# A macaron block's causal attention: the mask as a selection on GpSimd over the exponentials, diagonal units of equal width, values weighed in quarters, constants and first loads reordered

## The chip, the cores and the metric

One core of a Trainium2 chip runs the whole program. The metric is the device time of one launch in microseconds, the median over runs. Engines: TensorE (PE) multiplies, VectorE (DVE), ScalarE (ACT) and GpSimd (POOL) work on elements, and SyncE (SP) issues most DMAs. Each engine runs its own list of instructions in order; they wait for each other by semaphores.

## The reference

x has 4 sequences of 2048 rows of width 256. The block is x + 0.5 ffn(ln(x)), then + attention(ln(x)), then + 0.5 ffn(ln(x)); both feed-forward parts are a routed mixture of 8 experts and are not touched here. The attention, 16 heads of 16 with 4 nodes each:

```
node_probs = softmax(x @ Wr)                       # 4 nodes per head and row
pos = cumsum(node_probs) - node_probs              # positions for the rotation of q and k
scores = (q_r @ k_r.T) * SCALE + log(node_probs @ node_probs.T + 1e-08)
attn = softmax(where(causal, scores, -inf))        # key row <= query row
x + (attn @ v) @ Wo
```

The kernel takes the logarithm out of the softmax: exp(score) is multiplied by the sum over nodes of p_query * p_key. So the values are weighed beforehand by each of the 4 key nodes (`val`, 16 values and the weight itself, 17 columns per node, 68 per key row), and the 4 node sums are put together with the query's p afterwards.

## The kernel before

`build_attention` stands between two calls of `build_ffn`; nothing overlaps across them. 8192 rows are 64 tiles of 128, taken in pairs (TP = 32). Each pair goes through about ten steps per engine: normalise, transpose, project to v and node logits, softmax, sums before (positions), sine and cosine, rotate, split q and k in three bf16 parts, store these to DRAM, project the next q and k. Five pairs are made ahead, in `lead`; the others, and the output projections of finished rows, are slotted into the attention's unit loop at fixed steps of a *turn* (4 short turns of 24 units, then long ones of 40; the lists SHORT_AT and LONG_AT on each engine give the steps).

A *unit* is one head, 512 queries (CH = 4 tiles of 128) and two tiles of 128 keys. A head has 4 chunks of queries; chunk c has 2c full units and then two diagonal units, 20 units per head, 1280 in all, 512 of them diagonal. Scores are held keys down, queries across: tile `4c + t` of the keys meets the queries from t on, (4 - t) * 128 columns. Before, the first diagonal unit holds t = 0 and 1 (512 + 384 = 896 columns), the second t = 2 and 3 (256 + 128 = 384). A *visit* loads the q and k parts of two heads for chunks 0 and 1 (12 units), or of one head for chunks 2 and 3 (14 units); 96 visits.

For unit u: `scores(u)` on TensorE (L1568) fills `ring[u % 2]` in PSUM; on the first 128 columns of each diagonal tile two more matmuls (two halves of 64 keys) add -1e30 where the query is earlier than the key, as `ident_b` times `late_kq` (L1582 to L1585). `weights(u)` on ScalarE (L1181) writes the exponentials to `ew[u % 5]`. `weighted(u)` on TensorE (L1588) multiplies each 128 by 128 block of them with the 68 value columns, adding up a chunk in `mix[block % 2]`; each matmul here shows as two records in the trace, so a full unit has 32, the diagonal ones 28 and 12. `mix_nodes` on VectorE (L1435) finishes a chunk.

TensorE's order (L1778): at unit u it issues scores(u + 2), which waits for the exponentials of u, then weighted(u - 1), then the step of the turn. In a long turn, at step 0 and from step 26 (BURST) on, it also issues weighted(u), directly behind.

GpSimd (L1087) makes constants, `val` of the next visit (`weigh_values`, once per head and visit, at the visit's third unit) and the sums `acc`. Its constants are one chain; `consts_ready` is raised once, behind the last (L1110). VectorE, TensorE and ScalarE wait for it at their very start (L1295, L1565, L1163); ScalarE waits for all weights besides, scales Wq and Wk (L1168), loads the table and only then does `rsqrt(0)`. SP loads five weights, then the first x (L996 to L999).

Of the kernel before, what the change touches and what calls it, by code (L numbers as in the profile page):

```python
# [7 lines left out]
BF16 = mybir.dt.bfloat16  # L8
# [709 lines left out]
def build_attention(nc, x, Wq, Wk, Wv, Wr, Wo, q_parts, k_parts, B):  # L718
# [53 lines left out]
    for n, (v, e, i) in enumerate(stints):  # L772
# [10 lines left out]
    first_unit.append(U)  # L783
    block_of = [sum(1 for e in end_of if e < u) for u in range(U)]
# [17 lines left out]
    def place(u, n):  # L802

        n0, c, j, t0 = units[u]
        if j < CH * c:
            return 0, n * 512
        return (n, n * 512) if t0 == 0 else (2 + n, n * 256)

    def width(u):

        t, at = place(u, 1)
        return at + (CH - t) * P
# [31 lines left out]
    with ExitStack() as ctx:  # L844
# [15 lines left out]
        late_kq = sb("late_kq", [P, P], BF16)  # L860
# [69 lines left out]
        names = ("consts_ready pool_step dve_step act_step w_loaded w_scaled x_loaded var_ready rs_ready xn_ready xnT_ps "  # L930
# [60 lines left out]
        with nc.Block() as block:  # L991

            @block.sync
            def _(sp):
                sp.sem_inc(s["shift_loaded"], 32)
# [3 lines left out]
                sp.dma_start(xin[:, :, :], x_v[0]).then_inc(s["x_loaded"], 16)  # L999
# [88 lines left out]
            def _(pool):  # L1088
                ch = Chain(pool, s["pool_step"])
                identity(pool, ch, ident[:, :])  # L1090
                ch(pool.tensor_copy(ident_b[:, :], ident[:, :]))
                ch(pool.tensor_scalar(minus_b[:, :], ident[:, :], -1.0, None, ALU.mult))
# [3 lines left out]

                for m, a in ((late_kq, 1), (late_qk, -1)):
                    ch(pool.memset(m[:, :], 0.0))
                    ch(pool.affine_select(out=m[:, :], in_=m[:, :], compare_op=ALU.is_ge, fill=NEG,
                                          base=0, pattern=[[a, P]], channel_multiplier=-a))  # L1100
                ch(pool.memset(ones[:, :], 1.0))
                for f in range(NF):
                    ch(pool.memset(freq_t[:, f, :], freq[f]))
                    ch(pool.memset(cos1[:, f, :], float(np.cos(freq[f]) - 1.0)))
                    ch(pool.memset(sin1[:, f, :], float(np.sin(freq[f]))))
                ch(pool.memset(half_pi[:, :], PI / 2))
                for q in range(2):
# [21 lines left out]
                def weigh_visit(v):  # L1129
                    for n, (w, e, i) in enumerate(stints):  # L1130
                        if w == v:
                            weigh_values(n)
# [732 lines left out]
```

## Time and profile before

| | |
|---|---|
| median of 3 runs | 2971.42 us (2971.05 to 2972.08) |
| the profiled execution, its own time | 2976.97 us |
| its span in the profile | 2975.2 us |
| first ffn / start and lead of the attention / unit loop / second ffn | to 368 / to 562.4 / to 2594 / to 2975.2 us |
| busy: TensorE, VectorE, ScalarE, GpSimd | 2504.0, 1720.2, 1664.8, 644.3 us |

Times within the profile count from the start of the span. A group "x32" in a timeline merges instructions of one form that follow each other; "[0.40 <-PE ...]" is the idle time of the engine before it and what ended it. Matmuls overlap in the pipeline, so a mean duration is longer than the distance between two starts; the busy time of a group is the union. PEclk is the granted TensorE clock as a share of full speed.

### The profile page before, as it was taken

The page shows a single profiled execution, that of the slowest core. Times are in us where ns is not written, and L with a number is a line of the kernel's source. Part 1 is how long each engine was busy: PE and PEld are TensorE (multiplying, and loading weights), DVE is VectorE, ACT ScalarE, POOL GpSimd, SP SyncE. Part 2 cuts the span into 40 slices and gives each one's busy share as a digit, 9 for nine tenths or more (in the row PEclk, how much of TensorE's full clock was granted, in tenths as well). Part 3 has the DMA queues.
Part 4 walks back from the last instruction along what each step waited for, and adds up shares of the span by engine and source line. Part 5 has one row for each costly group of instructions (what it writes and reads, how often), then busy time and mean ns, then how long its engine had stood idle before and what let it go on. Part 6 is the DMA issues. An engine that isn't in the chain of part 4 may idle for free. (4 is left out here: it accounts for less than half of the span.)

```text
span 2975.2 us, 107297 instructions
## 1 busy us (share of the span) xinstructions
PE 2504.0 (84%) x48010; PEld 1968.7 (66%) x48012; DVE 1720.2 (58%) x3589; ACT 1664.8 (56%) x2102; POOL 644.3 (22%) x657
## 2 busy tenths in 40 slices
PE   7287535588899999999999989999999999962876
PEld 4155312366678888778888777888878888841554
DVE  7733158788666657767656776656575222267331
ACT  6022123355577777767777766777776666660221
POOL 1078710111011111111111111111111111010787
PEclk9598866799999999999999999999999999985988
DMA  6455501121212112211111221111122111161555
GB/s 226 134 102 102 79 29 30 47 60 40 58 52 60 45 51 73 69 48 56 56 52 51 78 64 52 59 52 48 58 75 65 46 46 46 44 234 25 98 101 75
DMA packets 185116, 207.46 MB, mean 70 GB/s; under 512 B 35984, under 2 KB 151712, under 8 KB 184480
## 3 DMA queue, kind: packets, MB, share of 16 engines
q1 hardware_dynamic: 158880, 165.60, 18.5%
q0 software_dynamic: 24576, 34.10, 7.2%
q8 instruction: 407, 6.67, 0.9%
q14 instruction: 101, 0.83, 0.1%
q10 hardware_dynamic: 1152, 0.26, 0.0%
HBM read 131.68 MB, written 76.02 MB: 70 GB/s over the span
## 5 line engine op out<-in xcount | busy, mean ns | idle before, releaser
L1186 ACT ACTIVATE at_ew<-at_ring 128x1024 f32<-128x1024 f32 (+2 forms) x1280 | 1114.9, 898 | 401.5 <-PE at_ring L1580 229.7
L1604 PEld LDWEIGHTS at_mix<-at_val,at_ew 128*64 128x64 f32 x34816 | 1210.0, 138 | 194.5 <-issue 43.2
L1604 PE MATMUL at_mix<-at_val,at_ew 128*64 128x68 f32 x34816 | 1258.9, 224 | 28.4 <-DVE at_mixed L1440 28.1
L1580 PE MATMUL at_ring<-at_qT,at_kT 98*64 98x512 bf16 (+3 forms) x5120 | 729.5, 352 | 55.5 <-ACT at_ew L1186 35.8
L1440 DVE TENSOR_TENSOR at_mixed<-at_mix,at_prob 128x272 f32<-128x272 f32 x256 | 112.4, 439 | 457.3 <-PE at_mix L1604 455.1
L1122 POOL TENSOR_TENSOR at_val<-at_prob,at_eps_t 128x32 f32<-128x32 f32 (+1 forms) x128 | 49.4, 386 | 1411.1 <-PE at_mix L1604 1411.1
L1580 PEld LDWEIGHTS at_ring<-at_qT,at_kT 98*64 98x64 bf16 x5120 | 255.8, 111 | 128.1 <-ACT at_ew L1186 45.5
L328 POOL DMA_INDIRECT out_dram<-ffn_xn,ffn_idx_all x128 | 212.6, 1661 | 53.2 <-issue 34.1
L1125 POOL TENSOR_TENSOR at_val<-at_vo,at_val 128x512 f32<-128x512 f32 (+1 forms) x128 | 211.4, 1652 | 10.0
L1660 PE MATMUL at_side<-at_w_all,at_turned 128*64 128x512 f32 (+1 forms) x1024 | 200.5, 536 | 11.9 <-ACT at_vo L1206 4.3
L1584 PE MATMUL at_ring<-at_late_kq,at_ident_b 128*64 128x128 bf16 x2048 | 204.9, 222 | 0.0
L318 POOL DMA_INDIRECT ffn_xn<-table,ffn_idx_all x128 | 123.2, 963 | 311.7 <-DMA ffn_idx_all<-ffn_idx_hi 273.6
L392 ACT ACTIVATE ffn_w1T<-ffn_pair 128x512 f32<-128x512 f32 x16 | 9.6, 597 | 297.0 <-PE ffn_pair L677 297.0
L1443 DVE TENSOR_REDUCE at_summed<-at_mixed 128x68 f32<-128x272 f32 x256 | 161.4, 630 | 8.8
L577 DVE TENSOR_SCALAR ffn_xn<-ffn_bank,ffn_slot_score 128x256 f32<-128x256 f32 x128 | 62.0, 484 | 177.5 <-PE ffn_bank L705 157.7
L1380 DVE TENSOR_REDUCE at_sums<-at_prods 128x512 f32<-128x2048 f32 x64 | 146.1, 2282 | 2.5 <-issue 1.2
L1660 PEld LDWEIGHTS at_side<-at_w_all,at_turned 128*64 128x64 f32 x1024 | 70.1, 144 | 104.4 <-issue 65.3
L1584 PEld LDWEIGHTS at_ring<-at_late_kq,at_ident_b 128*64 128x64 bf16 x2048 | 120.9, 113 | 7.5 <-issue 3.9
L697 PE MATMUL ffn_bank<-ffn_xn,ffn_w1T 128*128 128x512 f32 x256 | 120.7, 626 | 0.9 <-issue 0.9
L685 PE MATMUL ffn_pair<-ffn_ident,ffn_xn 128*128 128x128 f32 x256 | 50.5, 377 | 79.7 <-DMA ffn_xn<-table,ffn_idx_all 79.1
L705 PE MATMUL ffn_bank<-ffn_w2T,ffn_xn 128*128 128x256 f32 x512 | 116.8, 384 | 0.0
L1445 DVE TENSOR_TENSOR at_vo<-at_summed,at_recip 128x64 f32<-128x64 f32 x256 | 111.2, 434 | 8.8
(227 smaller groups left out, 2790.3 us busy)
## 6 DMA issues: line engine op xcount, KB each, us to landing
table<-ffn_xn SPq DMA_DIRECT2D x32, 512.0 KB, 6.3
q_parts<-at_parts SPq DMA_DIRECT2D x64, 192.0 KB, 2.5
k_parts<-at_parts SPq DMA_DIRECT2D x64, 192.0 KB, 3.0
at_qT<-q_parts SPq DMA_DIRECT2D x128, 96.0 KB
at_kT<-k_parts SPq DMA_DIRECT2D x64, 192.0 KB
ffn_front<-in_L_attn_x_dram SPq DMA_DIRECT2D x16, 512.0 KB, 5.5
ffn_w_in<-in_L_ffn_w_dram SPq DMA_DIRECT2D x32, 256.0 KB, 3.7
at_xin<-out_dram SPq DMA_DIRECT2D x32, 256.0 KB, 5.4
```

Of the source, the lines that this page charges most:

```text
L318: pool.indirect_dma_start(out=rows[e % 2][:, j, :], out_offset=None, in_=table, in_offset=bass.IndirectOffsetOnAxis(ap=idx_all[:, e * J + ...
L328: pool.indirect_dma_start(out=dst, out_offset=bass.IndirectOffsetOnAxis(ap=idx_all[:, e * J + j:e * J + j + 1], axis=0), in_=y[e % 2][:, j ...
L697: last = pe.matmul(bank[n % 2][:, :], w1T[q][:, k, f * P:(f + 1) * P], xeT[:, k, s * 512:(s + 1) * 512], start=(k == 0), stop=(k == DK - 1))
L705: last = pe.matmul(bank[2 + j % 2][:, 0:D], hT[:, f, j * P:(j + 1) * P], w2T[q][:, f, :], start=(f == 0), stop=(f == FK - 1))
L1125: pool.tensor_tensor(val[q][:, tiles, :, 0:HD], vv.unsqueeze(2).to_broadcast([P, nk, K, HD]), val[q][:, tiles, :, HD].unsqueeze(3).to_broa ...
L1186: act.activation(ew[u % NE_BUF][:, 0:w], ring[u % 2][:, 0:w], ACT.Exp).then_inc(s["exp_ready"], 1)
L1380: ch(dve.tensor_reduce(sums[:, n:n + 2, :].rearrange("p c n -> p (c n)"), prods[:, n:n + 2, :].rearrange("p c (n k) -> p (c n) k", k=K), A ...
L1443: ch(dve.tensor_reduce(summed[:, :, :], mixed[:, :, :, :].rearrange("p t k w -> p t w k"), AX.X, ALU.add))
L1580: lastm = pe.matmul(ring[u % 2][h:h + HALF, at:at + w], kT[q][:, kc + n * P + h:kc + n * P + h + HALF], qT[q][:, qc + t * P:qc + 512], sta ...
L1584: lastm = pe.matmul(ring[u % 2][h:h + HALF, at:at + P], ident_b[:, h:h + HALF], late_kq[:, :], start=False, stop=True)
L1604: lastm = pe.matmul(mix[block_of[u] % 2][h:h + HALF, t * K * VW:(t + 1) * K * VW], ew[u % NE_BUF][:, col + h:col + h + HALF], val[q][:, ti ...
L1660: lastm = pe.matmul(side[h:h + HALF, g * 512:g * 512 + n], turned[0][:, g * DK + k, h:h + HALF], w_all[:, k, first:first + n], start=(k == ...
```

## The change

- `late_kq` and its 2048 matmuls go. `mask_late(u)` on GpSimd waits for the exponentials of a diagonal unit and sets to 0, in one selection over two pieces of 128 columns in `ew`, those with the query before the key. It raises `masked`.
- The diagonal units hold t = 0 and 3 (columns 0 to 640) and t = 1 and 2 (columns 128 to 768), 640 columns each. `weighted` does the blocks off the diagonal first, then waits for `masked` and does the two on it.
- Values are weighed for four key tiles at a time (256 columns), at four units of the visit before; the node weights of all its heads come ahead of the first quarter.
- Constants: `consts_ready` rises three times: identity; then `before`, `ones`, the frequency constants (without waits between them), `half_pi`, `ident_b`, `minus_b`; last `eps_t`, the rows of `qT` and `kT`, and `late_qk`. Each engine waits where it first needs one. ScalarE loads its table first and does `rsqrt(0)` ahead of the weights. SP issues x first.

```diff
-            units += [(n, c, 2 * p, 0) for p in range(2 * c)] + [(n, c, CH * c, 0), (n, c, CH * c + 2, 2)]
+            units += [(n, c, 2 * p, None) for p in range(2 * c)] + [(n, c, CH * c, (0, 3)), (n, c, CH * c, (1, 2))]
...
+    def tile_pair(u):
+        n0, c, j, late = units[u]
+        if late is None:
+            return [(j + n, 0, n * 512) for n in range(2)]
+        return [(j + t, t, at) for t, at in zip(late, (0, 512) if late == (0, 3) else (P, 512))]
...
 SP:
+                sp.dma_start(xin[:, :, :], x_v[0]).then_inc(s["x_loaded"], 16)
                 sp.sem_inc(s["shift_loaded"], 32)
...
-                sp.dma_start(xin[:, :, :], x_v[0]).then_inc(s["x_loaded"], 16)
...
 GpSimd:
+                ch(pool.memset(ident[:, :], 0.0))
+                pool.affine_select(out=ident[:, :], in_=ident[:, :], compare_op=ALU.not_equal, fill=1.0,
+                                   base=0, pattern=[[-1, P]], channel_multiplier=1).then_inc(s["consts_ready"], 1)
...
+                pool.tensor_scalar(minus_b[:, :], ident[:, :], -1.0, None, ALU.mult).then_inc(s["consts_ready"], 1)
...
+                def mask_late(u):
+                    pool.wait_ge(s["exp_ready"], u + 1 + PRIME_S)
+                    at, size = (0, 512) if units[u][3] == (0, 3) else (P, 384)
+                    late = ew[u % NE_BUF][:, at:at + 2 * size].rearrange("p (n c) -> p n c", c=size)[:, :, 0:P]
+                    pool.affine_select(out=late, in_=late, compare_op=ALU.is_ge, fill=0.0,
+                                       base=0, pattern=[[0, 2], [1, P]], channel_multiplier=-1).then_inc(s["masked"], 1)
...
                 def unit(u, at, short, new, fin, post):
-                    if u - 2 in first_unit:
-                        v = first_unit.index(u - 2) + 1
-                        if 1 < v < V:
-                            weigh_visit(v)
+                    if u in late_of:
+                        mask_late(u)
+                    v = visit_of[u] + 1
+                    part_at = (2, 3, 8, 9) if len(visits[v - 1][0]) == 2 else (2, 3, 7, 9)
+                    if 1 < v < V and u - first_unit[v - 1] in part_at:
+                        part = part_at.index(u - first_unit[v - 1])
+                        if part == 0:
+                            weigh_nodes(v)
+                        weigh_values(v, part)
...
 ScalarE:
-                act.wait_ge(s["w_loaded"], 16 * 5)
-                act.wait_ge(s["consts_ready"], 1)
                 act.sem_inc(s["exp_ready"], PRIME_S)
+                act.preload_act_table_set("natural_log_exp_and_others")
...
+                rsqrt(0)
+                act.wait_ge(s["w_loaded"], 16 * 5)
...
 TensorE, weighted(u):
+                    whole = [(j, t, at + (t - first) * P) for j, first, at in tile_pair(u) for t in range(first + late, CH)]
+                    for n, (j, t, col) in enumerate(whole):
+                        lastm = add(j, t, col, begin and n == 0, False)
+                    if late:
+                        pe.wait_ge(s["masked"], late_of[u] + 1)
+                        for n, (j, t, at) in enumerate(tile_pair(u)):
+                            lastm = add(j, t, at, False, u in end_of and n == 1)
```

## Rows read from the trace of the kernel before

**Rows 1.** Busy us by stretch: PE, PEld, DVE, ACT, POOL, PEclk, DMA share, GB/s

```profile
562.40:771.40 209.00, 167.26 (x3218) 130.08 (x3220) 163.20 (x315) 116.33 (x157) 27.23 (x33) 0.91 0.19 54
771.40:2236.50 1465.10, 1436.69 (x32663) 1179.71 (x32661) 981.35 (x1827) 1061.08 (x1284) 197.26 (x226) 0.99 0.20 58
2236.50:2594.00 357.50, 352.66 (x8999) 306.29 (x8996) 97.87 (x205) 243.82 (x275) 45.21 (x40) 1.00 0.17 48
```

**Rows 2.** Waits of PE in 762 to 2594: us, times, longest

```profile
PE at_mix L1604 <- DVE at_mixed L1440: 28.1, 17, 5.2
...
PE at_ring L1580 <- ACT at_ew L1186: 3.2, 6, 1.0
```

**Rows 3.** Timeline of the attention's start: start us, us, engine, line, operation

```profile
368.43 0.20 POOL L49 MEMSET at_ident<- 128x128 f32 x1 [6.66 <-POOLq L228]
...
370.98 0.47 SPq L999 DMA_DIRECT2D at_xin<-out_dram  x1
...
383.75 0.10 POOL L1110 MEMSET at_eps_t<- 128x1 f32 x1
...
383.97 1.33 ACT L1168 ACTIVATE at_w_all<-at_prods 128x256 f32<-128x256 f32 x4 [41.07 <-POOL at_eps_t L1110]
...
385.08 0.17 DVE L1306 TENSOR_SCALAR at_var<-at_mv 128x2 f32<-128x2 f32 x1
...
386.85 0.20 ACT L1179 ACTIVATE at_rs<-at_logv 128x2 f32<-128x2 f32 x1
...
388.76 1.09 PE L1652 MATMUL at_side<-at_ident,at_xn 128*128 128x128 f32 x4 [39.36 <-DVE at_xn L1319]
389.89 0.60 ACT L1195 ACTIVATE at_turned<-at_side 128x512 f32<-128x512 f32 x1 [2.83 <-PE at_side L1652]
```

**Rows 4.** Groups by form: busy us, mean ns, idle before

```profile
L1186 ACT ACTIVATE at_ew<-at_ring 128x896 f32<-128x896 f32 x256 | 235.4, 919 | 90.4 <-PE at_ring L1584 90.0
...
L1584 PE MATMUL at_ring<-at_late_kq,at_ident_b 128*64 128x128 bf16 x2048 | 204.9, 222 | 0.0
...
L1099 POOL TENSOR_SCALAR_AFFINE_SELECT at_late_kq<-at_late_kq 128x128 bf16<-128x128 bf16 x1 | 0.3, 292 | 0.1
```

**Rows 5.** Timeline of PE at one pair of diagonal units

```profile
1502.06 0.22 PE L1584 MATMUL at_ring<-at_late_kq,at_ident_b 128*64 128x128 bf16 x2
1502.12 0.33 PE L1580 MATMUL at_ring<-at_qT,at_kT 98*64 98x384 bf16 x2
...
1503.40 0.22 PE L1584 MATMUL at_ring<-at_late_kq,at_ident_b 128*64 128x128 bf16 x2
1503.46 0.22 PE L1580 MATMUL at_ring<-at_qT,at_kT 98*64 98x128 bf16 x2
```

**Rows 6.** Timeline: exponentials and value product of a diagonal unit in a burst

```profile
1139.09 1.30 ACT L1186 ACTIVATE at_ew<-at_ring 128x896 f32<-128x896 f32 x2
...
1140.52 1.00 PE L1604 MATMUL at_mix<-at_val,at_ew 128*64 128x68 f32 x28
```

**Rows 7.** Timeline: GpSimd beside two operations of VectorE

```profile
1201.38 2.29 DVE L1374 TENSOR_TENSOR at_prods<-at_cs,at_g_t 128x2048 f32<-128x2048 f32 x1
...
1201.78 1.99 POOL L1122 TENSOR_TENSOR at_val<-at_prob,at_eps_t 128x32 f32<-128x32 f32 x1 [14.22 <-PE at_mix L1604]
...
1203.70 2.29 DVE L1380 TENSOR_REDUCE at_sums<-at_prods 128x512 f32<-128x2048 f32 x1
...
1203.85 1.10 POOL L1125 TENSOR_TENSOR at_val<-at_vo,at_val 128x512 f32<-128x512 f32 x1
...
1204.90 0.25 POOL L1122 TENSOR_TENSOR at_val<-at_prob,at_eps_t 128x32 f32<-128x32 f32 x1
```

**Rows 8.** Timeline: L1445 on VectorE alone, and beside a GpSimd product

```profile
1141.56 0.23 DVE L1445 TENSOR_TENSOR at_vo<-at_summed,at_recip 128x64 f32<-128x64 f32 x1
...
1509.04 2.02 POOL L1125 TENSOR_TENSOR at_val<-at_vo,at_val 128x1024 f32<-128x1024 f32 x1
...
1509.97 1.18 DVE L1445 TENSOR_TENSOR at_vo<-at_summed,at_recip 128x64 f32<-128x64 f32 x1
```

More of the change, by code:

```diff
@@ L783, in build_attention @@
     first_unit.append(U)
+    visit_stint = [n for n, (v, e, i) in enumerate(stints) if e == 0]
+    visit_of = [stints[n][0] for n, c, j, late in units]
     block_of = [sum(1 for e in end_of if e < u) for u in range(U)]
@@ L800, in blocks_until, with columns, vals_until @@
         return 1 + max(block_of[u] for u in end_of if stints[units[u][0]][2] // H == b and units[u][1] == c)
[L802 to L812, printed above, removed]
+    def tile_pair(u):
[3 more added lines that the diff above has]
+        return [(j + t, t, at) for t, at in zip(late, (0, 512) if late == (0, 3) else (P, 512))]
+    def columns(u):
+        first, last = tile_pair(u)
+        return first[2], last[2] + (CH - last[1]) * P
+    late_of = {u: n for n, u in enumerate(u for u in range(U) if units[u][3] is not None)}
+    def vals_until(stint):
+        return sum(1 + shape_of(v)[3] // CH for v, e, i in stints[:stint])
     NP = max(len(p) for p in pieces)
@@ L1095, in _ @@
                                       base=0, pattern=[[1, P]], channel_multiplier=-1))
[L1097 to L1100, printed above, removed]
                 ch(pool.memset(ones[:, :], 1.0))
                 for f in range(NF):
-                    ch(pool.memset(freq_t[:, f, :], freq[f]))
-                    ch(pool.memset(cos1[:, f, :], float(np.cos(freq[f]) - 1.0)))
-                    ch(pool.memset(sin1[:, f, :], float(np.sin(freq[f]))))
+                    ch.add(pool.memset(freq_t[:, f, :], freq[f]))
+                    ch.add(pool.memset(cos1[:, f, :], float(np.cos(freq[f]) - 1.0)))
+                    ch.add(pool.memset(sin1[:, f, :], float(np.sin(freq[f]))))
                 ch(pool.memset(half_pi[:, :], PI / 2))
+                pool.wait_ge(s["consts_ready"], 1)
+                ch(pool.tensor_copy(ident_b[:, :], ident[:, :]))
+                pool.tensor_scalar(minus_b[:, :], ident[:, :], -1.0, None, ALU.mult).then_inc(s["consts_ready"], 1)
+                ch(pool.memset(eps_t[:, :], EPS))
                 for q in range(2):
@@ L1150, in unit @@
                 def unit(u, at, short, new, fin, post):
[L1151 to L1154 removed]
+                    if u in late_of:
[5 more added lines that the diff above has]
+                        if part == 0:
+                            weigh_nodes(v)
+                        weigh_values(v, part)
                     if at == (10 if short else 14) and new is not None:
@@ L1598, in weighted, with add @@
                         pe.wait_ge(s["u_taken"], block_of[u] + 1)
[L1599 to L1608 removed]
+                    def add(tile, t, col, first, last):
+                        for h in range(0, P, HALF):
+                            m = pe.matmul(mix[block_of[u] % 2][h:h + HALF, t * K * VW:(t + 1) * K * VW],
+                                          ew[u % NE_BUF][:, col + h:col + h + HALF],
+                                          val[q][:, tile0 + tile, :, :].rearrange("p k w -> p (k w)"),
+                                          start=first, stop=last, skip_group_check=True)
+                        return m
+                    late = u in late_of
+                    whole = [(j, t, at + (t - first) * P) for j, first, at in tile_pair(u) for t in range(first + late, CH)]
[5 more added lines that the diff above has]
+                            lastm = add(j, t, at, False, u in end_of and n == 1)
                     lastm.then_inc(s["av_done"], 1)
```

102 lines of the change are left out of this document (43 added, 59 removed).

## The prediction

> **What bounds the kernel now.** I read the stretches first. The attention's unit loop is 562.4 to 2594.0, two thirds of the span. TensorE is busy for 1436.7 of 1465.1 us in its middle and for 352.7 of 357.5 at its end; ScalarE there is at 72% and 68%, VectorE at 67% and 27% [rows 1]. The list of waits says what its pauses from 762 on are: 28.1 us for VectorE and 3.2 us for exponentials [rows 2]. So in 771.4 to 2594.0 a TensorE instruction that goes away shortens the kernel by its pitch. The loop's head, 562.4 to 771.4 (the four short turns), is another case: TensorE has 167 busy us of 209, VectorE 163, and the two wait for each other through ScalarE [rows 1]. Third, 368.4 to 388.8 in the timeline: over 20 us before the attention's first matmul, in most of which GpSimd alone works [rows 3].
>
> **The start of the attention.** Before: GpSimd makes its constants one after another from 368.43 until the memset of `eps_t` ends at 383.85, and only that releases ScalarE (383.97) and VectorE [rows 3]. The four memsets of `qT` and `kT` hold it last. Input x is issued sixth, at 370.98. Then: statistics, weight scaling and a table load ahead of rsqrt (done 387.05), normalisation, first transposes 388.76 [rows 3].
> After: x is issued first, near 368.5. Its issue row at 370.98 shows it behind five weights; I let it land by 372.3, an estimate that leaves 3.8 us. Statistics end 1.4 us after their release (383.85 to 385.25), rsqrt is two instructions like the one of 0.20, 0.45 together, with the table already loaded, normalisation runs from 387.05 to 388.76, 1.7 us [rows 3]. That gives transposes at about 375.8, done at 376.9. Beside it ScalarE waits for five weights, whose last issue stays at about 371.0; with 4.4 us for issue and landing (estimate) it scales until 376.8, and copies the transposed tile then. Both arms meet near 376.8 where before they met at 389.9. **Gain 13 us.** Bounds 10 (a landing 3 us later) and 15 (neither arm late). `before`, `ident_b` and `half_pi` come by about 376 and are wanted 12 us later; the last constants (the four memsets, then `late_qk`) by about 385 and are wanted at the first visit, 150 us later. What is late next is the weights' landing. The five lead steps behind it are one chain, shift as a whole, and keep their length. SP's other DMAs keep order.
>
> **TensorE loses the mask matmuls.** Per pair of diagonal units four tiles take a second accumulation: 256 pairs, 2048 matmuls. Their mean of 222 ns is not their price [rows 4]: they are pipelined, and the two halves of a tile run together. From start to start: 1502.06 to 1502.12 and 1503.40 to 1503.46, so 0.06 us for two [rows 5]; 128 columns at the upper clock level, 2.4 GHz, which rows 1 show granted (0.99 and 1.00), say 0.053. I take 0.057. 1024 pairs come to 58 us. 64 of the 512 diagonal units lie in the four short turns (7.3 us), where TensorE does not bound; I credit half, 3.6. The rest, 51.1 us, is credited whole. Score columns and value matmuls stay as many: 512+384 and 256+128 columns become twice 640, exponentials too. Two halves alike should even ScalarE's pace; with 3.2 us of waits for exponentials left [rows 2] I price that at nothing.
>
> **GpSimd gets 512 selections.** The nearest row is a selection over 128 columns, 292 ns [rows 4]. Twice 128 columns are wanted: at least 0.29, twice that is 0.58, and a two-input operation over 512 columns, 1.10 us when free, is the far end. I take 0.45, near the first, since the fixed part is paid once.
> Does TensorE wait for it? The changed value product does its unmasked blocks first. I measured in the timeline, for every diagonal unit, the time from its exponential's end to where the last 8 value records start. Outside bursts TensorE is a unit behind: 337 units, at least 1.7 us, medians 3.4 and 3.9. In bursts (step 26 on and step 0 of a long turn) 175 units, least 1.07, median 2.05. The least: the 896-wide exponential that starts 1139.09 ends 0.92 later at 1140.01; its 28 value records start 1140.52 and take 1.0, so the last eight start near 1141.1 [rows 4, 6]. The shorter scores and the smaller unit take about 0.25 off. 0.45 plus two handovers of about 0.1 fits in 0.85: undisturbed, no unit waits.
> Disturbed it does. A GpSimd operation that meets `L1374` on VectorE is held: `L1122`, 0.25 us when free, took 1.99 from 1201.78 until L1374 was over; beside the reduction L1380 the 512-column operation took its free 1.10 [rows 7]. L1374 (2.29 us) runs twice in a row per long turn, at step 30, in the burst. In the 23 long turns that have it 24 diagonal exponentials end inside it and too late for 0.5 us of masking; their overdue times add to 22.5 us, and with neighbours that share one stall I count **15 us lost**. Bounds: 0 (other alignment, since all that follows is earlier) and 47 (0.8 us a selection, 0.6 us less slack: 50 units late).
> On this the Trainium skill, page "SBUF — State Buffer" (section "SBUF: two separate sides"), says: VectorE operations with two SBUF inputs or in a two-port mode and GpSimd operations hold a shared port pair exclusively, and the loser blocks fully. The trace agrees (1.99 against 0.25). By a split of bandwidth instead, the loss would be near 0 and the sum 15 us lower.
> It works both ways: `L1445` took 1.18 us instead of 0.23 while a GpSimd product ran [rows 8]. 512 selections of 0.45 with a third of VectorE's time in such operations delay VectorE by some 30 us in all, of which 7 in the short turns. Where TensorE bounds, VectorE has 480 us spare [rows 1]: free. In the short turns I charge 4, and 2 at the turns where value sums of short rows make TensorE wait for L1440. Bounds 0 and 15.
>
> **Queues.** In GpSimd's queue a selection can stand behind a quarter of the values (256 columns, about 0.64 by 0.18 + 0.46, from 1.10 and 2.02 for 512 and 1024 [rows 7, 8]). The quarters lie at steps 2, 3 and 7, 8 or 9 of a visit, which are full units, so no selection is due beside them; extra fixed costs, 4 times 0.2 a visit, are GpSimd's own: it is 13% busy [rows 1], with the selections some 25%. `add_up` stands behind the selection of its unit. The node weights wait for the previous visit's last product, behind the selections that this product needs: no circle. Values are ready by step 10 and wanted at 12 or 14. All nothing; if the quarters came late, a visit's start would wait, 94 times.
>
> **Sum**, against the profiled execution: 2976.97 - 13 - 3.6 - 51.1 + 15 + 6 = 2930.3. The median of the runs shown is 5.5 lower, 2971.42, so about 2925, 1.6% less.
>
> **Rivals.**
> (a) *Only the start gains.* The mask matmuls hid in TensorE's shadow, ScalarE or VectorE set the pace, or stalls eat it all: 2971.4 - 13, about 2958. For it: VectorE at 67% and the exclusion. Against it: TensorE's 98 and 99% [rows 1].
> (b) *Slower: the selection itself outlasts the slack.* At 0.9 us 6 units wait, at 1.6 63 (25 us), at 2.0 161 (78), at 2.5 208 (168), without VectorE's holds. It decides from about 1.8 us, where stalls reach the 64 us of gain less the holds; at 2.5, with 512 selections barring VectorE too, 2971 - 68 + 168 + 20 gives about 3090; at 2.0 about 3000. Against it: 292 ns for half the columns.
> (c) *No stalls*: 2971.4 - 71, about 2901, if GpSimd slips between or L1374 rarely meets a diagonal.
>
> **Numbers.** Main 0.66, with its own range 2912 to 2940; (c) 0.12; (a) 0.15; (b) 0.07. A measurement here tells 0.2%, 6 us, from no change. Faster by more: main, (c), most of (a), 0.87; within: 0.06, the far end of (a), where stalls also take the start's gain; slower 0.07. Range 2900 to 2960.
>
> **What will show it.** First attention transposes near 376 instead of 388.8. No L1584. The loop from 771 on about 36 to 50 us shorter, the short turns as long as before within 5. Selections of 0.4 to 0.5 us, some stretched to 2 or more beside L1374; TensorE's new waits on them in the bursts, some 20 of a microsecond. Wrong if selections average over 0.8 us, if TensorE's waits for them exceed 40 us, if ScalarE's waits for scores vanish (it would then bound), or if the start still waits for GpSimd.

## The result and the profile after

The changed kernel takes 2936.30 us (median of 4 runs, 2933.87 to 2937.91); the kernel before, beside it on the same chip, 2971.75 us. The ratio is 0.9876 with the interval 0.9859 to 0.9893: 1.2% or some 35 us less, where 46 were forecast. The profiled execution after has 2933.87 us against 2976.97 before, 43 us apart. It lies 2.4 below its median and that of before 5.2 above the median of 2971.75, so some 8 us of what the profiles differ by is scatter between executions.

The same stretches after (columns as in [rows 1]): the four short turns, the middle of the unit loop, its end; then one plain turn, and the two turns 10 and 11, in which new rows are brought in.

```profile
555.80:756.60 200.80, 157.50 (x2962) 120.11 (x2964) 164.00 (x315) 116.89 (x156) 77.42 (x112) 0.92 0.20 56
756.60:2203.70 1447.10, 1399.48 (x31233) 1138.52 (x31231) 981.19 (x1827) 1066.62 (x1285) 447.77 (x767) 0.99 0.20 58
2203.70:2549.20 345.50, 341.14 (x8613) 294.59 (x8611) 85.44 (x204) 247.09 (x275) 90.82 (x185) 1.00 0.17 49
883.30:945.20 61.90, 61.90 (x1407) 50.47 (x1403) 37.27 (x69) 47.79 (x56) 16.20 (x29) 1.00 0.20 57
...
1125.90:1191.10 65.20, 57.83 (x1241) 46.65 (x1243) 52.82 (x106) 42.04 (x57) 27.72 (x49) 0.97 0.28 80
1191.10:1258.50 67.40, 57.58 (x1237) 46.38 (x1233) 51.55 (x106) 42.31 (x57) 28.21 (x47) 0.95 0.18 51
```

The same three turns of the kernel before:

```profile
901.50:965.10 63.60, 63.60 (x1461) 52.25 (x1459) 39.47 (x71) 47.68 (x57) 7.68 (x8) 1.00 0.19 55
...
1149.60:1211.50 61.90, 58.66 (x1341) 48.39 (x1341) 48.26 (x103) 41.90 (x58) 11.42 (x15) 1.00 0.27 80
1211.50:1281.50 70.00, 61.26 (x1340) 50.55 (x1342) 52.80 (x109) 42.62 (x56) 9.30 (x11) 0.95 0.19 52
```

The plain turn loses 1.7 us, all of it TensorE's work. Turns 10 and 11 lose TensorE's work too (58.66 to 57.83, 61.26 to 57.58 us), but together they are longer: 132.6 us against 131.9. Their GpSimd time rises from 20.7 to 55.9 us and VectorE's from 101.1 to 104.4.

TensorE's waits in 755 to 2550 (us in all, times, longest), to compare with [rows 2]:

```profile
PE at_mix L1620 <- DVE at_mixed L1466: 30.1, 14, 5.3
PE at_mix L1620 <- POOL at_ew L1125: 12.2, 11, 1.7
...
PE at_ring L1602 <- ACT at_ew L1204: 1.5, 2, 0.7
```

The selections by form, beside the value products (busy us, mean ns, idle before):

```profile
L1125 POOL TENSOR_SCALAR_AFFINE_SELECT at_ew<-at_ew 128x256 f32<-128x256 f32 x512 | 292.6, 576 | 1078.2 <-ACT at_ew L1204 1077.2 <-DVE at_prob L1358 0.6
L1147 POOL TENSOR_TENSOR at_val<-at_vo,at_val 128x256 f32<-128x256 f32 x384 | 266.6, 715 | 7.5
```

The durations of the 512 selections (shortest, median and longest, in ns):

```profile
L1125 POOL TENSOR_SCALAR_AFFINE_SELECT at_ew<-at_ew x512: 398/407/2493, 557.3 to 2547.9; 128x256 f32<-128x256 f32 x171
```

A free selection takes 0.41 us, as the median does; the mean is 0.58, since some take up to 2.5 us. The start, in the timeline (start us, us), answers to [rows 3]:

```profile
368.52 0.38 SPq L1002 DMA_DIRECT2D at_xin<-out_dram  x1
...
371.36 0.75 DVE L1326 BATCH_NORM_STATS2 at_stats<-at_xin 128x6 f32<-128x256 f32 x2 [2.52 <-DMA at_xin<-out_dram]
...
372.00 1.80 POOL L1114 MEMSET at_qT<- 2x2048 bf16 x1
...
372.43 1.40 DVE L1331 TENSOR_SCALAR at_var<-at_mv 128x2 f32<-128x2 f32 x1
373.86 1.80 POOL L1115 MEMSET at_kT<- 2x2048 bf16 x1
...
374.53 0.16 DVE L1338 TENSOR_TENSOR at_rs<-at_rs,at_var 128x2 f32<-128x2 f32 x1
374.73 0.96 DVE L1339 TENSOR_SCALAR at_rs<-at_rs 128x2 f32<-128x2 f32 x1
...
375.92 3.64 DVE L1344 TENSOR_SCALAR at_xn<-at_xin,at_mv,at_rs 128x256 f32<-128x256 f32 x2
...
379.71 1.09 PE L1677 MATMUL at_side<-at_ident,at_xn 128*128 128x128 f32 x4 [30.11 <-DVE at_xn L1344]
381.48 4.53 PE L1685 MATMUL at_side<-at_w_all,at_turned 128*64 128x320 f32 x16 [0.69 <-ACT at_turned L1220]
```

The statistics begin at 371.36, so the input lands sooner than estimated. The first transposes start at 379.71, 9.05 us earlier than before, and not at 376: VectorE's one-tensor operations stretch while GpSimd's memsets run (1.40 for 0.17 in [rows 3]), its two-tensor operation between them does not (0.16).

### The profile page after: what moved, and what is told of

It is laid out like the page before. It is cut to its first block and busy times, and to the rows that moved or that the text cites. A ratio compares the mean times of both kernels' runs of the same rounds, so it can differ in the third digit from the quotient of the medians.

```text
span 2931.7 us, 104032 instructions
## 1 busy us (share of the span) xinstructions
PE 2448.4 (84%) x45962; PEld 1906.9 (65%) x45964; DVE 1713.1 (58%) x3589; ACT 1674.4 (57%) x2102; POOL 990.4 (34%) x1423
## 5 line engine op out<-in xcount | busy, mean ns | idle before, releaser
L1620 PEld LDWEIGHTS at_mix<-at_val,at_ew 128*64 128x64 f32 x34816 | 1223.5, 138 | 240.7 <-issue 36.1
L1204 ACT ACTIVATE at_ew<-at_ring 128x1024 f32<-128x1024 f32 (+1 forms) x1280 | 1125.2, 898 | 361.1 <-PE at_ring L1602 355.1
L1620 PE MATMUL at_mix<-at_val,at_ew 128*64 128x68 f32 x34816 | 1262.7, 224 | 45.0 <-DVE at_mixed L1466 30.1
L1602 PE MATMUL at_ring<-at_qT,at_kT 98*64 98x512 bf16 (+3 forms) x5120 | 698.7, 352 | 55.7 <-ACT at_ew L1204 36.2
L1125 POOL TENSOR_SCALAR_AFFINE_SELECT at_ew<-at_ew 128x256 f32<-128x256 f32 x512 | 292.6, 576 | 1078.2 <-ACT at_ew L1204 1077.2
L1602 PEld LDWEIGHTS at_ring<-at_qT,at_kT 98*64 98x64 bf16 x5120 | 228.7, 111 | 109.1 <-ACT at_ew L1204 48.3
L1147 POOL TENSOR_TENSOR at_val<-at_vo,at_val 128x256 f32<-128x256 f32 x384 | 266.6, 715 | 7.5
L328 POOL DMA_INDIRECT out_dram<-ffn_xn,ffn_idx_all x128 | 212.9, 1663 | 53.2 <-issue 34.1
L705 PEld LDWEIGHTS ffn_bank<-ffn_w2T,ffn_xn 128*128 128x128 f32 x512 | 90.6, 189 | 30.3 <-issue 17.7
L685 PEld LDWEIGHTS ffn_pair<-ffn_ident,ffn_xn 128*128 128x128 f32 x256 | 44.6, 199 | 84.6 <-DMA ffn_xn<-table,ffn_idx_all 83.0
```

Source lines behind the costliest of these rows:

```text
L328: pool.indirect_dma_start(out=dst, out_offset=bass.IndirectOffsetOnAxis(ap=idx_all[:, e * J + j:e * J + j + 1], axis=0), in_=y[e % 2][:, j ...
L705: last = pe.matmul(bank[2 + j % 2][:, 0:D], hT[:, f, j * P:(j + 1) * P], w2T[q][:, f, :], start=(f == 0), stop=(f == FK - 1))
L1125: pool.affine_select(out=late, in_=late, compare_op=ALU.is_ge, fill=0.0, base=0, pattern=[[0, 2], [1, P]], channel_multiplier=-1).then_inc ...
L1147: pool.tensor_tensor(val[q][:, tiles, :, 0:HD], vv.unsqueeze(2).to_broadcast([P, CH, K, HD]), val[q][:, tiles, :, HD].unsqueeze(3).to_broa ...
L1204: act.activation(ew[u % NE_BUF][:, a:b], ring[u % 2][:, a:b], ACT.Exp).then_inc(s["exp_ready"], 1)
L1602: lastm = pe.matmul(ring[u % 2][h:h + HALF, at:at + (CH - t) * P], kT[q][:, kc + j * P + h:kc + j * P + h + HALF], qT[q][:, qc + t * P:qc ...
```

## The experiments

The stages by which the profiles are compared, in us (worked out from each trace: "start" is the attention's first constant to the first transposes, "lead" from there to the first score matmul; a turn counts from the exponentials of its first unit, 0.8 to 1.2 us behind the first score matmul in the first turn; "short" is the four short turns, "six" the turns 10, 11, 18, 19, 26 and 27, in which new rows are brought in, "other" the remaining long turns, "loop" the sum of these three):

```
                  start  lead   short  six    other   loop    span
before            20.3   173.6  207.7  384.2  1438.5  2030.4  2975.2
after             11.2   176.1  200.0  387.8  1405.6  1993.4  2931.7
start_only        11.2   175.2  207.4  384.6  1438.9  2030.8  2967.5
no_mask_matmuls   20.3   177.5  204.4  378.9  1405.7  1989.0  2935.6
select_aside      11.2   176.2  200.8  390.8  1403.6  1995.2  2929.2
no_select         11.2   175.8  200.4  380.7  1404.0  1985.2  2921.2
spread_steps      11.2   176.4  200.0  396.0  1403.1  1999.0  2956.2
old_widths        11.2   175.7  203.9  391.4  1412.5  2007.8  2961.6
values_at_once    11.2   175.8  202.4  385.1  1410.9  1998.3  2955.5
memsets_on_dve    10.3   175.5  202.1  387.5  1405.9  1995.5  2949.3
after_again       11.2   175.2  202.2  391.2  1405.9  1999.3  2955.7
memsets_later      6.3   176.6  201.9  388.1  1406.5  1996.4  2949.4
diag_behind       11.2   173.6  201.1  399.8  1414.1  2015.0  2969.9
all_three          6.4   176.1  200.8  396.7  1414.5  2011.9  2967.5
```

From spread_steps on, the runs are on two other chips, where the parts outside the attention take some 20 us more (the kernel before: 2994.59 and 2997.12 us), so across groups the ratios and the stages are compared, not the spans. The stages scatter too: "loop" of the one changed kernel is 1993.4 and 1999.3, "six" 387.8 and 391.2.

The changed kernel's "loop" is 37.0 us shorter than before: 7.7 in the short turns and 29.3 in the long ones.

For the six turns, the busy time of two engines and the time at 1.2 GHz by the granted clock, in us (a stretch at 0.90 of the clock spends a fifth of its time at 1.2 GHz):

```
                 length  TensorE busy  VectorE busy  at 1.2 GHz
before            384.2         352.7         281.9        20.5
no_mask_matmuls   378.9         337.3         283.8        22.9
after             387.8         339.3         291.9        30.7
after_again       391.2         340.8         293.0        34.1
select_aside      390.8         345.5         293.7        44.4
no_select         380.7         338.8         284.4        30.7
spread_steps      396.0         348.3         297.0        47.4
old_widths        391.4         344.6         293.7        41.0
diag_behind       399.8         349.6         295.7        44.4
```

**start_only.** The kernel before with the new start alone.

```diff
+ sp.dma_start(xin[:, :, :], x_v[0])...        # ahead of the weights
+ rsqrt(0)                                      # ahead of the weights' scaling
+ pool: ident, before, freq_t.., eps_t, memsets of qT/kT, late_kq, late_qk
```

> The kernel before, with the constants and first loads in the new order and nothing else; the mask stays two matmuls per diagonal tile. Theory: the start alone is worth what the two traces show up to the first attention transposes, 388.76 against 379.71, 9.1 us, less about 2.5 us that the first projections lose at the lower clock level: 6 to 9 us, ratio 0.997 to 0.998. Rival 1 (my recorded step): 13 us, ratio 0.9956. Rival 2: the five lead steps absorb it: 0 to 2 us.

Measured: 2969.43 us beside 2973.81, ratio 0.9983 (0.9973 to 0.9993): 4 to 5 us, a little under the 6 to 9 expected. The stage is 9.1 us shorter, and the loop unchanged, 2030.8 against 2030.4. So the start gains by itself, 4 us less in its stage than the 13 of the prediction, and in this trace the lead is 1.6 us longer. The same holds are in this trace:

```profile
371.81 1.39 DVE L1308 TENSOR_SCALAR at_var<-at_mv 128x2 f32<-128x2 f32 x1
...
374.10 0.96 DVE L1316 TENSOR_SCALAR at_rs<-at_rs 128x2 f32<-128x2 f32 x1
```

**no_mask_matmuls.** The kernel before without the 2048 mask matmuls.

```diff
-                        if late:
-                            for h in range(0, P, HALF):
-                                lastm = pe.matmul(ring[...], ident_b[:, h:h + HALF], late_kq[:, :], start=False, stop=True)
```

> The kernel before with the 2048 mask matmuls left out, so the causal mask inside the diagonal tiles is left out. Theory: 0.057 us for each of 1024 pairs, of which the 64 diagonal units of the short turns give half: about 55 us, 50 to 58, ratio 0.981. Rival 1: the matmuls hide in the pipeline and are worth under 35 us (0.989), which would explain the whole of the changed kernel's gain without any cost of the selections. Rival 2: ScalarE or VectorE takes over as the bound: 40 us and new waits for exponentials.

Measured: 2934.83 us, ratio 0.9872 (0.9854 to 0.9889), 38 us and not 55, which is what Rival 2 said. "Other" takes 1405.7 against 1438.5, 32.8 us less; before, 1156 of the mask matmuls started in these turns, and 578 pairs at 0.057 are 32.9. There the price was right to 1%. In "six" only 5.3 us came, where 636 matmuls, 318 pairs, should give 18.1. TensorE's busy time there did fall by 15.4 us (352.7 to 337.3), but its idle time grew by 10. TensorE's waits for VectorE in this kernel's loop say where most of that went:

```profile
PE at_mix L1600 <- DVE at_mixed L1440: 35.7, 21, 5.3
```

They were 28.1 in [rows 2], and the waits for exponentials grew from 3.2 to 5.8. VectorE's busy time in "six" did not shrink with TensorE's (281.9 and 283.8): its work in these turns has its own length.

**select_aside.** The changed kernel with each selection run on a tile of its own, so that TensorE never waits for one; the mask does not reach the exponentials.

```diff
-                    late = ew[u % NE_BUF][:, at:at + 2 * size]...[:, :, 0:P]
+                    late = aside[:, :, :]
-                        pe.wait_ge(s["masked"], late_of[u] + 1)
...
```

Here and in no_select TensorE also waits for the exact count of weighed values that a head needs; no wait of TensorE for `val` is in the list of either.

> The changed kernel, but each selection works on a tile of its own of the same size, and TensorE doesn't wait for it, so the mask inside the diagonal tiles is left out. GpSimd keeps the same load on VectorE. Theory: TensorE's waits for GpSimd (12.2 us in the trace) and the clock dips after them go: 12 to 18 us faster than the changed kernel, 2918 to 2924. Rival: the cost of the selections is mostly their hold on VectorE: then under 5 us faster, and the run without selections gives the rest.

Measured: 2932.28 us, ratio 0.9869 (0.9854 to 0.9884), the same as with the waits, where 12 to 18 us were expected. The 12.2 us of waits for selections are gone, those for VectorE grew from 30.1:

```profile
PE at_mix L1624 <- DVE at_mixed L1470: 38.2, 16, 5.5
```

"Six" is no shorter (390.8). Taking the waits away alone gains nothing: 8 of the 12 us are now waited for VectorE. The rest is less clear. In "six" TensorE's idle time is 3 us less than in the changed kernel, but its busy time 6 us more, with 44.4 us at 1.2 GHz instead of 30.7. No run shows whether the lower clock follows from the moved waits.

**no_select.** The changed kernel with no selection at all; the mask is left out.

```diff
-                    pool.affine_select(out=late, in_=late, compare_op=ALU.is_ge, fill=0.0, ...).then_inc(s["masked"], 1)
+                    pool.sem_inc(s["masked"], 1)
```

> The changed kernel with the selections left out but the handover kept: GpSimd waits for each diagonal unit's exponentials and raises the semaphore that TensorE waits for; the mask inside the diagonal tiles is left out. Theory: 2 to 6 us faster than the run with selections aside, since VectorE's holds cost little where TensorE bounds: 2914 to 2920. Rival (VectorE's holds are the cost): 10 to 20 us faster than the run aside. If the handover itself cost, this run would be slower than the one aside.

Measured: 2921.73 us, ratio 0.9831 (0.9817 to 0.9844): 11 us less than select_aside, 13 less by the ratio of the changed kernel. The loop is 8 to 10 us shorter, nearly all in "six" (380.7 against 387.8 and 390.8). That is the expectation's rival. The waits were gone in both kernels; only here are the operations gone. So what the selections cost comes with the operations and not with TensorE's waits for them. That it comes through VectorE fits the traces: VectorE is busy 1689.8 us of the span instead of 1713.1, and 284.4 instead of 291.9 in "six"; the short turns lose VectorE work too and are no shorter (200.4 and 200.0). Against select_aside the clock has a part in it, since 6.7 of the 10.1 us in "six" are TensorE's busy time (338.8 against 345.5). Against the changed kernel it has none: both were at 1.2 GHz for 30.7 us, and TensorE idles 6.6 us less. Turns 10 and 11 of this kernel, VectorE third of the busy times:

```profile
1127.70:1192.10 64.40, 57.62 (x1242) 47.08 (x1244) 51.96 (x107) 42.08 (x58) 13.40 (x21) 0.97 0.28 80
1192.10:1258.70 66.60, 57.86 (x1238) 46.75 (x1235) 49.90 (x105) 42.30 (x57) 11.51 (x20) 0.95 0.18 52
```

101.9 us of VectorE instead of 104.4, 131.0 us for the two turns instead of 132.6.

**spread_steps.** The two node products of a long turn and what follows them drawn apart on VectorE.

```diff
-                LONG_AT = (1, 2, 5, 8, 10, 14, 17, 20, 22, 30, 32, 25, 34, 33)
+                LONG_AT = (1, 2, 5, 8, 10, 14, 17, 20, 22, 30, 34, 25, 38, 36)   # second product at unit 32
```

> The changed kernel, with VectorE's last steps of a long turn moved apart: node products in two (units 30 and 32), sums at 34 and 38, normalisation at 36, instead of 30, 32, 34 and 33. Theory: in the six long turns of chunks 0 and 1 (10, 11, 18, 19, 26, 27; 387.7 us in the changed kernel) TensorE waits for VectorE to empty the value sums, up to 5.3 us behind this block of steps; spread, the waits of about 30 us fall below half and these turns shorten by 10 to 25 us, the others stay: 2912 to 2926. Rival 1 (TensorE's waits for the selections are the cost): the two products apart shorten a selection's longest wait, the 12 us fall, but the six turns keep their waits for VectorE: 2925 to 2932. Rival 2: the next turn's first steps then wait for the later sums: slower than the changed kernel.

Measured: 2961.98 us, ratio 0.9896 (0.9876 to 0.9915), no faster: a miss. Beside memsets_on_dve on the same chip it is 10.7 us slower. The 5.3 us wait at unit 38 of turn 11 fell to 1.9, and this turn is 3.5 us shorter (63.9 for 67.4). But the work pushed back from the end of a turn arrives at the head of the next. Waits of turn 10 in the changed kernel, then here (1133.0 to 1204.5), and then its stretch:

```profile
PE at_mix L1620 <- DVE at_mixed L1466: 4.4, 3, 1.7
...
PE at_mix L1622 <- DVE at_mixed L1466: 6.1, 3, 2.5
...
1133.00:1204.50 71.50, 62.44 (x1243) 50.98 (x1245) 56.45 (x113) 42.62 (x58) 28.12 (x48) 0.90 0.24 68
```

71.5 us against 65.2, and 0.90 of the granted clock against 0.97: of 71.5 us some 14 at 1.2 GHz, where the changed kernel has 3.4. The two waits at the turn's head grew only from 1.7 and 1.2 us to 2.5 and 2.0; TensorE's busy time grew by 4.6 (62.44 for 57.83). Turn 10 lost 6.3 us where turn 11 gained 3.5.

**old_widths.** The changed kernel with the diagonal units as wide as before, 896 and 384 columns.

```diff
-            units += [...] + [(n, c, CH * c, (0, 3)), (n, c, CH * c, (1, 2))]
+            units += [...] + [(n, c, CH * c, (0, 1)), (n, c, CH * c, (2, 3))]
...                                             # tile_pair and mask_late with the matching columns
```

> The changed kernel with the diagonal units as before: 896 and 384 columns, tiles 0 and 1, then 2 and 3. Theory: equal widths matter in the four short turns alone, where the changed kernel gained 7.8 us and the leaving out of the matmuls alone 3.5: 3 to 6 us slower than the changed kernel, 2939 to 2942. Rival 1: nothing, within 2 us (the quarters of the values made that difference). Rival 2: the second unit has a single block ahead of its masked ones and TensorE's waits for GpSimd double: over 10 us slower.

Measured: 2965.83 us, ratio 0.9907 (0.9888 to 0.9926) against 0.9876 and 0.9868 for the changed kernel. Expected were 3 to 6 us, all in the short turns; more came, as Rival 2 said, and most of it in the long ones. The loop is 2007.8, against 1995.5 of memsets_on_dve on the same chip and 1999.3 of after_again: 8 to 12 us. "Other" alone has 6.6 of it, where after, after_again, memsets_on_dve and memsets_later lie within 0.9 (1405.6 to 1406.5). The waits:

```profile
PE at_mix L1620 <- POOL at_ew L1125: 15.7, 17, 1.7
PE at_ring L1602 <- ACT at_ew L1204: 4.7, 13, 1.0
```

TensorE waits for selections 17 times rather than 11, and 13 times for an exponential before the next scores rather than 2. The equal widths, priced at nothing, are the second gain of the change. But most of it is there only beside the selections: without any, the kernel with equal widths (no_select) and the one with the old ones (no_mask_matmuls) differ by 3.8 us in the loop (1985.2 and 1989.0, on one chip), all in the short turns.

**values_at_once.** All four value quarters of a visit issued at its unit 2.

```diff
-                    part_at = (2, 3, 8, 9) if len(visits[v - 1][0]) == 2 else (2, 3, 7, 9)
+                    if 1 < v < V and u - first_unit[v - 1] == 2: weigh_visit(v)
```

> The changed kernel with all values of a visit weighed at its third unit, as before. Theory: the quarters are worth little, since selections are due before and after: 0 to 4 us slower than the changed kernel, as selections of units 4 and 5 stand behind 2 us of products. Rival: one long hold on VectorE is cheaper than four: up to 3 us faster. A second rival: over 10 us slower, if TensorE meets the late selections in every visit.

Measured: 2951.72 us, ratio 0.9859 (0.9838 to 0.988), no different from the changed kernel. Waits for selections rise to 20.0 us, those for VectorE fall to 19.4:

```profile
PE at_mix L1616 <- POOL at_ew L1125: 20.0, 14, 2.6
PE at_mix L1616 <- DVE at_mixed L1462: 19.4, 13, 4.7
```

The one change cancels the other: beside memsets_on_dve on the same chip "other" is 5.0 us longer and "six" 2.4 shorter. The quarters bring nothing that can be measured in the kernel's time.

**memsets_on_dve.** The four memsets of `qT` and `kT` issued by VectorE before the input lands.

```diff
-                    ch(pool.memset(qT[q][KQ:KS, :], 0.0))
+                    ch.add(dve.memset(qT[q][KQ:KS, :], 0.0))
```

> The changed kernel with the four memsets of qT and kT issued by VectorE while it waits for x, instead of GpSimd. Theory: GpSimd's memsets held VectorE's single-tensor operations at the start (1.40, 0.96 and 3.64 us where 0.17, 0.17 and 0.73 were needed): first transposes 3 to 4 us earlier, at 375.5 to 376.5, and the end as much earlier, 2932 to 2934, unless the projections behind lose it at the lower clock level. Rival: VectorE's memsets take as long as GpSimd's 1.8 us each, 7 us in all, and the transposes come later than 380.

Measured: 2951.29 us, ratio 0.9857 (0.9836 to 0.9879), the start 0.9 us shorter, where 3 to 4 were expected. The holds are gone, and VectorE's own memsets, 6.3 us from the first's start to the last's end, keep the statistics back:

```profile
379.11 0.91 DVE L1320 MEMSET at_qT<- 2x1024 uint32 x1 [0.27 <-issue]
...
383.61 1.76 DVE L1321 MEMSET at_kT<- 2x2048 bf16 x1 [0.38 <-issue]
385.41 0.75 DVE L1327 BATCH_NORM_STATS2 at_stats<-at_xin 128x6 f32<-128x256 f32 x2
386.20 0.25 DVE L1330 BATCH_NORM_AGGREGATE at_mv<-at_stats 128x2 f32<-128x6 f32 x2
386.48 0.17 DVE L1332 TENSOR_SCALAR at_var<-at_mv 128x2 f32<-128x2 f32 x1
```

**after_again.** The changed kernel once more, beside the last group.

> The changed kernel itself once more, with five rounds beside the kernel before. Expected 0.9876 again, within 0.9859 to 0.9893, since only the runs above it differ in chip and phase. It is the measure for the three others of this group. In the trace its six turns of chunks 0 and 1 should take 385 to 390 us and the others 1405 to 1407.

Measured: 2955.90 us beside 2997.12, ratio 0.9868 (0.9853 to 0.9883). The waits for selections repeat to the decimal (12.2, 11 times), those for VectorE nearly (31.4 for 30.1), and "other" too (1405.9). "Six", 391.2, is 3.4 us longer than in the first trace and over the 385 to 390 expected: that much is scatter, and it goes in part with the clock (34.1 us at 1.2 GHz for 30.7).

**memsets_later.** The changed kernel with one wait on GpSimd ahead of the four memsets.

```diff
+                pool.wait_ge(s["xn_ready"], 1)
```

> The changed kernel, with GpSimd holding its four memsets of qT and kT back until VectorE has normalised the first pair; VectorE is then idle for 6.8 us until the first logits. Theory: what the start was short of my 13 us are the holds of these memsets on VectorE's single-tensor operations: first transposes 3.5 to 4 us earlier, 7.3 us after the start of the attention instead of 11.2, and 3 to 4 us off the time of the changed kernel. Rival: the projections behind them run longer at the lower clock level and take it back: 0 to 1 us.

Measured: 2948.52 us, ratio 0.9845 (0.9829 to 0.9862), 7.4 us under after_again, of which the start gives 4.9. The intervals of the two ratios overlap; the stage itself, 11.2 in nine traces and 6.3 and 6.4 in the two with this edit, does not. By its ratio it is the fastest of the kernels that compute the whole reference. The three held operations take their free time:

```profile
384.61 0.17 DVE L1332 TENSOR_SCALAR at_var<-at_mv 128x2 f32<-128x2 f32 x1
...
385.67 0.17 DVE L1340 TENSOR_SCALAR at_rs<-at_rs 128x2 f32<-128x2 f32 x1
...
386.07 0.73 DVE L1345 TENSOR_SCALAR at_xn<-at_xin,at_mv,at_rs 128x256 f32<-128x256 f32 x2
386.84 0.37 SPq L1038 DMA_DIRECT2D at_xin<-out_dram  x1
...
386.93 1.80 POOL L1115 MEMSET at_qT<- 2x2048 bf16 x1 [2.83 <-DVE at_xn L1345]
```

The Trainium skill, page "SBUF — State Buffer" (section "SBUF: two separate sides"), tells two conflicts apart: a VectorE operation with two SBUF inputs is kept out only by a GpSimd operation that reads SBUF, one in a two-port mode by any. A memset reads nothing; that it held the one-tensor operations (1.40, 0.96, 3.64 for 0.17, 0.17, 0.73) and not the two-tensor one (0.16) agrees, if the held ones ran in a two-port mode, which no row here shows.

**diag_behind.** In the bursts the value product of a diagonal unit is put a unit later.

```diff
-                        weigh_until(u)
+                        weigh_until(u - 1 if u in late_of else u)
```

> The changed kernel, with TensorE one unit behind on diagonal units in bursts too, so that a selection has a unit more of time. Theory: TensorE's waits for GpSimd (12.2 us) vanish, but most of them stand in the six turns where VectorE's lateness takes their place: 2 to 4 us faster, the turns 9, 17, 25 by 0.8 each. Rival 1 (the waits are the selections' cost): 10 to 14 us faster. Rival 2: ScalarE gets its buffers later and its waits rise: slower.

Measured: 2972.63 us, ratio 0.9919 (0.9901 to 0.9937), 16.7 us slower than after_again where 2 to 4 faster were expected: a miss. The waits for selections did fall, those for VectorE and for exponentials grew:

```profile
PE at_mix L1620 <- DVE at_mixed L1466: 37.2, 15, 5.6
PE at_mix L1620 <- POOL at_ew L1125: 5.7, 7, 1.2
...
PE at_ring L1602 <- ACT at_ew L1204: 3.6, 11, 0.5
```

"Six" lost 8.6 us and "other" 8.2, in 24 turns, 0.3 each on average. In "six" the loss stands in TensorE's busy time (349.6 for 340.8), with 44.4 us at 1.2 GHz for 34.1. In "other", that it comes from exponentials whose scores are now issued later (ScalarE waits 185.0 us for the scores of the diagonal units, after 165.5) is argued, not shown; no run separates it.

**all_three.** memsets_later, diag_behind, and each node product of VectorE in two halves.

```diff
+                        for a in range(2):
+                            ch.add(dve.tensor_tensor(prods[:, n + a, :]..., cs[:, a, :]..., w..., ALU.mult))
```

> The changed kernel with the memsets later, diagonal units one behind in bursts, and each of VectorE's two node products of 4.6 us together issued in two halves, so that a selection is held for 1.2 us instead of 2.3. Theory: 4 us from the start and 3 to 6 from the loop, 7 to 10 us faster than the changed kernel. Rival: the halves cost VectorE fixed time in the turns where it is the bound, and only the start is left: 4 us.

Measured: 2967.02 us, ratio 0.9903 (0.9888 to 0.9919), slower than either memsets_later or after_again, where 7 to 10 us less were expected: a miss. Against diag_behind it is 5.6 us faster, of which the start gives 4.8, so the halves are worth little. TensorE's list of waits has one of 0.3 us for a selection, and 44.5 us for VectorE:

```profile
PE at_mix L1622 <- DVE at_mixed L1468: 44.5, 19, 6.0
```

## Why the prediction was right, and where it was not

The time was right (2936 for 2925, inside the main case's own range), but partly by luck, since errors cancelled. The forecast for the loop was 54.7 less 21, 33.7 us; 37.0 came in the first trace and 31.1 in after_again. It fits worse by parts. The forecast had nothing to gain in the short turns (3.6 less 4), and 7.7 and 5.5 came; it had 34.1 in the long ones (51.1 less 15 and 2), and 29.3 and 25.6 came, less than the 36 to 50 that the prediction named as a sign.

1. *The start, 13 us.* Measured 9.1 in the stage. The step that was off is "normalisation runs from 387.05 to 388.76, 1.7 us", taken over together with the free durations of the small operations: moved beside the four memsets, they take 3.64 for the normalisation and 2.0 more in two small ones. memsets_later takes this away and gets to 6.3 us from the first constant, 14 less than before. The prediction had moved the memsets off the path and then priced them as if they did nothing to their neighbour, though it used the same hold for the selections. "The five lead steps behind it ... keep their length" holds within the scatter: the lead is 1.6 to 2.5 us longer in the first traces, but it also reads 177.5 in no_mask_matmuls, whose lead is the code of before, and 173.6, as before, in diag_behind. TensorE's projections there run partly at 1.2 GHz (0.69 granted in 379.1 to 390.0 of start_only), which may be what varies.
2. *The mask matmuls in the short turns, 3.6.* Measured 3.3 (no_mask_matmuls). Right.
3. *"The rest, 51.1 us, is credited whole."* This is the term that was mis-sized: no_mask_matmuls gives 38.1 in the long turns. 32.8 came in full where TensorE bounds; 12.8 of 18.1 were lost in the six turns where rows are brought in. In the first two of them TensorE had 119.9 of 131.9 us busy before, and its pauses are nearly all waits for VectorE, which is busy 101.1 us with operations of up to 2.3 us. One average over 771.4 to 2236.5 [rows 1] hid this: 98% is the mean of turns at up to 100% and of some at 95 and 88%. Per turn, it stands in the same view.
4. *"Two halves alike should even ScalarE's pace ... I price that at nothing."* Worth 8 to 12 us beside the selections (old_widths) and 3.8 without them. The 3.2 us of waits for exponentials [rows 2] may have been only what lasted long enough to be listed; no run shows that.
5. *TensorE waits for selections, 15 us lost, 20 times.* 12.2 us, 11 times. The place was right: all eleven stand beside or at most 0.4 us behind the node products in the burst. The duration of a free selection was right too, 0.41 for 0.45. One such place:

```profile
1177.30 2.29 DVE L1400 TENSOR_TENSOR at_prods<-at_cs,at_prob 128x2048 f32<-128x2048 f32 x1 [0.63 <-issue]
1179.51 2.49 DVE L1400 TENSOR_TENSOR at_prods<-at_cs,at_g_t 128x2048 f32<-128x2048 f32 x1
```

```profile
1177.67 5.31 POOL L1125 TENSOR_SCALAR_AFFINE_SELECT at_ew<-at_ew 128x256 f32<-128x256 f32 x4 [6.88 <-ACT at_ew L1204]
```

```profile
1179.91 0.46 PE L1620 MATMUL at_mix<-at_val,at_ew 128*64 128x68 f32 x8 [1.44 <-POOL at_ew L1125]
...
1182.32 0.72 PE L1620 MATMUL at_mix<-at_val,at_ew 128*64 128x68 f32 x8 [1.32 <-POOL at_ew L1125]
```

   Four selections take 5.31 us, over three times their free 1.6, and the last eight matmuls of two units wait. But these waits are not what the selections cost: without them nothing was gained (select_aside), without the selections 11 to 13 us (no_select).
6. *VectorE's delays, 6 us, of which 4 in the short turns.* This is where the cost of the selections seems to be, 8 to 10 us in the loop, and it is in the six turns, not in the short ones (200.4 without selections, 200.0 with). VectorE's delays add to 23 us (1713.1 for 1689.8 busy) where the prediction had 30. The total of steps 5 and 6, 21 us, was too much by 11 to 13 against the loop, by 8 to 10 against the kernel's time.
7. *Queues, nothing.* Held: quarters or all at once make no difference (values_at_once).

The 37.0 us of the loop can be taken apart by no_mask_matmuls and no_select: 41.4 by the mask matmuls (before against no_mask_matmuls), 3.8 by the widths and quarters without selections (no_mask_matmuls against no_select), less 8.2 by the selections (no_select against the changed kernel). At the old widths the selections would cost 18.8 (old_widths against no_mask_matmuls, on two chips, so give or take 6): by these traces the equal widths about halve their price. These are differences between the same traces that give the 37.0, so their sum proves nothing; each part stands on its own run.

Of the rivals, (a) falls with the loop's 37 us. (c) falls with the 12.2 us of waits, and no_select, 2921.7 us with no selection at all, does not reach its 2901 either. (b) falls with selections of 0.41 us free and 1.7 us for the longest wait.

## What to carry to other kernels

Read utilisation turn by turn before crediting a removed instruction whole: a stretch at 98% can be turns at 100%, which pay in full, and a few at about 90%, which paid under a third here. Work moved to a free GpSimd is paid where VectorE is tight; take both the wait and the operation away in turn to see which one costs, and read the granted clock beside each result, since it can take back what a shorter wait gives. A memset that is off the critical path still belongs behind the short operations that are on it.

## What the hardware showed unexpectedly

- A GpSimd memset over two partitions (1.80 us) held VectorE's one-tensor operations until it ended, one of 0.17 us for 1.40, and let a two-tensor operation of the same size through in 0.16.
- Moving a wait can cost more than the wait. In spread_steps a wait of 5.3 us fell to 1.9, two at the head of a turn grew from 1.7 and 1.2 to 2.5 and 2.0, and the granted clock of that turn fell from 0.97 to 0.90. In all, TensorE had 51 us at 1.2 GHz in the long turns, where the changed kernel has 34 and 41 in its two traces. With select_aside and diag_behind it was 51 too, and neither was faster for its fewer waits for selections. That the moved waits lower the clock is not shown apart.
- A GpSimd selection over 128 partitions and twice 128 f32 columns took 0.41 us when free, and up to 2.49 beside VectorE's products of two tensors.
- The memset of 2x2048 bf16 on VectorE took 0.91 us for one value and 1.76 for the other: the first was run as 1024 elements of uint32.
